# The first attention with its key and query weights multiplied on the chip, the second norm and the logits one round sooner, and more unread products between gate and experts

## The reference

```python
x = x + tanh(g_xattn[0]) * xattn0(layernorm(x), ctx)      # q = n Wq + bq, k = ctx Wk + bk, v = ctx Wv + bv
                                                          # softmax(q k^T) v, one head, width 256
x = x + tanh(g_ffn[0])   * moe(layernorm(x))              # logits of 12, the best 2; 8 experts (256 -> 512 -> 256, silu),
                                                          # 4 "zero" experts that hand the row on
x = x + tanh(g_xattn[1]) * xattn1(layernorm(x), ctx)      # 16 heads of 16, then Wo
x = x + tanh(g_ffn[1])   * fp8_linear(layernorm(x))
```

## Time and profile before

| | |
|---|---|
| three runs | 387.19, 388.37, 388.74 us |
| the profiled execution | 389.65 us |
| its span, first to last instruction | 387.8 us |
| mean granted clock of PE | 0.972 of 2.4 GHz |
| PE, DVE, ACT, POOL busy | 350.9, 266.2, 223.2, 159.3 us |

### The profile page before, as it was taken

One profiled execution on the slowest core, in us unless ns is written; L12 is line 12 of the kernel. 1 busy time (PEld: TensorE's weight loads), 2 busy tenths in 40 slices (PEclk: granted clock), 3 DMA queues, 4 the chain that ended last, 5 costly groups with the idle time before them and its releaser, 6 DMA issues.

```text
span 387.8 us, 9156 instructions
## 1 busy us (share of the span) xinstructions
PE 350.9 (90%) x2992; PEld 277.5 (72%) x2993; DVE 266.2 (69%) x678; ACT 223.2 (58%) x462; POOL 159.3 (41%) x215
## 2 busy tenths in 40 slices
PE   1989999877899999999999999889999999989874
PEld 1778787645799999999999983657666666656642
DVE  1559779893645665555544567867888998685995
ACT  2488798511444455444554442566677778737694
POOL 7397599504355555565555444321133023010000
PEclk9999999975999999999999999989999999999997
DMA  7998662301133334323232214211011000000014
GB/s 201 305 416 356 275 246 84 109 2 54 46 104 102 128 95 135 104 72 81 68 79 73 66 56 137 95 57 50 8 57 56 2 2 2 3 2 2 0 56 163
DMA packets 15387, 38.26 MB, mean 99 GB/s; under 512 B 3574, under 2 KB 4748, under 8 KB 13820
## 3 DMA queue, kind: packets, MB, share of 16 engines
q1 hardware_dynamic: 9978, 22.55, 16.6%
q0 software_dynamic: 3936, 10.45, 9.3%
q10 hardware_dynamic: 1442, 4.85, 3.2%
HBM read 24.34 MB, written 13.50 MB: 98 GB/s over the span
## 4 chain that ended last, share of the span: by engine, by line
PE 71%; DVE 10%; ACT 7%; DMA 6%; issue 3%; ACTq 1%; SPq 1%; POOL 0%; DVEq 0%
PE two L1747 14%; PE two L1760 14%; PE two L1896 5%; PE two L1926 4%; PE two L1779 4%; PE two L1961 4%; PE two L1882 4%; PE two L1862 3%; DMA x_sb<-in_x 3%; PE two L1770 2%; PE two L1953 2%; PE two L1613 1%; DMA bq_sb<-in_bq 1%; PE two L1942 1%; PE two L1630 1%
## 5 line engine op out<-in xcount | busy, mean ns | idle before, releaser
L1226 DVE SCALAR_TENSOR_TENSOR gate<-th,two 128x512 f32<-128x512 f32 x39 | 26.8, 687 | 59.6 <-ACT th L742 34.1
L742 ACT ACTIVATE th<-two 128x512 f32<-128x512 f32 x39 | 23.3, 599 | 73.0 <-PE two L1760 40.2
L549 POOL DMA_INDIRECT y_d<-y_sb,goal_i x39 | 38.5, 986 | 50.6 <-ACT y_sb L752 50.6
L543 POOL DMA_INDIRECT xg<-xn_d,slot_i x39 | 37.9, 971 | 33.5 <-DVE slot_i L1179 13.8
L1747 PE MATMUL two<-wh,gh 128*128 x156 | 44.2, 283 | 0.1
L1747 PE MATMUL two<-wh,gl 128*128 x156 | 44.0, 282 | 0.0
L1747 PE MATMUL two<-wl,gh 128*128 x156 | 43.8, 281 | 0.0
L563 POOL TENSOR_TENSOR rstd<-var,half 128x2 f32<-128x2 f32 x14 | 9.8, 701 | 76.9 <-DVE var L1293 76.9
L1326 DVE TENSOR_REDUCE nm<-two 128x8 f32<-128x960 f32 x32 | 36.1, 1152 | 5.3 <-PE two L1882 5.0
L516 POOL TENSOR_TENSOR wl<-wl,wh 128x512 fp32r<-128x512 f32 x28 | 35.3, 1278 | 8.5 <-ACT wh L671 8.5
L1760 PE MATMUL two<-wh,xh 128*128 x78 | 35.0, 449 | 1.8 <-DVE xl L1220 1.8
(11 more groups left out here) (273 smaller groups left out, 883.1 us busy)
## 6 DMA issues: line engine op xcount, KB each, us to landing
wl<-in_wmoe SPq DMA_DIRECT2D x8, 1024.0 KB, 14.4
y_d<-wh ACTq DMA_DIRECT2D x4, 1024.0 KB
yg<-y_d SPq DMA_DIRECT2D x7, 512.0 KB, 3.5
xn_d<-xq SPq DMA_DIRECT2D x8, 256.0 KB, 2.0
xz<-xn_d SPq DMA_DIRECT2D x8, 256.0 KB
out_x<-of SPq DMA_DIRECT2D x8, 256.0 KB, 2.0
x_sb<-in_x SPq DMA_DIRECT2D x1, 1024.0 KB, 11.6
x_sb<-in_x SPq DMA_DIRECT2D x1, 768.0 KB, 4.5
```

The costliest lines, as they stand in the source:

```text
L543: pool.indirect_dma_start(xg[:, n % 2, :], None, xn_d, bass.IndirectOffsetOnAxis(ap=slot_i[:, n:n + 1], axis=0)).then_inc(gathered[n % 2], 16)
L549: pool.indirect_dma_start(y_d, bass.IndirectOffsetOnAxis(ap=goal_i[:, n:n + 1], axis=0), y_sb[:, n % 2, :], None).then_inc(y_stored[n % 2] ...
L742: nc.scalar.activation(th[:], bank[2 + k][:], ACT.Tanh, scale=0.5).then_inc(th_ok, 1)
L1226: dve.scalar_tensor_tensor(gate[:, k, :], th[:], 1.0, bank[2 + k][:], ALU.add, ALU.mult).then_inc(gate_ok, 1)
```

## The change

In the first attention the key and query weights are multiplied once at the start (`fold_keys`: transpose of `wk0`, its product with `wq0` and `bq0`, and the products of the biases). `keys0` then makes the keys of all eight batches in four products of 480 columns and two of one row; DVE (`copy_kq0`) and ACT (`copy_kq1`) keep them before round 1. `keys_by_query`, `copy_kt0`, `copy_kq` and `copy_bqk` go. The loops have `B + 6` rounds (DVE's starts at -4) where they had `B + 9`; the second norm stands two or three rounds behind the attention step as before, and its logits one round nearer. The pieces of the weights are dealt out by the tables `HIGHS`, `LOWS` and `VECTOR_LOW`, and DVE takes five of the rests, not four. The transfers that clear `y_d` move from ACT's list to SP's, behind the seventh of the eight weight transfers. In routing 7 unread products come behind the last value products, one behind each of the first three groups of slot products, and 5 where 3 stood. One unread product stands in the second attention before PE waits for `oT_ok`.

```diff
-        VECTOR_LOW, VECTOR_FROM = (7, 10, 13, 16), 5
-        LOW_LATE = {B: 3, B + 1: 4, B + 2: 3, B + 3: 2, B + 4: CHUNKS}
+        HB = B // 2 * LK
+        HIGHS = 0, 2, 3, 3, 2, 2, 2, 2, 3, 3, 3, 3, 2, 2
+        LOWS = (1, 2, 2, 2, 2, 2, 2)
+        VECTOR_LOW = 2, 5, 8, 11, 13
...
                 sp.dma_start(wl[:, c].bitcast(F32), wmoe[:, c]).then_inc(chunk_in[m], 16)
+                if m == LOADS - 2:
+                    sp.wait_ge(zero_ok, 1)
+                    sp.dma_start(xn_d[0:1, :], wh[0:1, E_FFN * WE - D:].bitcast(F32)).then_inc(zeroed, 16)
+                    y_p = y_d[1:1 + 2 * TILES * P, :].rearrange("(p r) n -> p (r n)", p=P)
+                    for c in range(0, 2 * TILES * D, ZEROS):
+                        sp.dma_start(y_p[:, c:c + ZEROS], wh[:, E_FFN * WE - ZEROS:].bitcast(F32)).then_inc(zeroed, 16)
...
+            for b in range(4):
+                root0(b)
+            low_next(1)
+            root0(4)
+            root0(5)
+            for b in range(6, B):
+                low_next(2)
+                root0(b)
+            low_next(1)
+            for b in range(B):
+                if b:
+                    low_next(LOWS[b - 1])
+                root1(b)
...
-            def copy_kt0(b):
...
+            def copy_kq1():
+                act.wait_ge(fold_ok, 3)
+                for h in range(2):
+                    act.wait_ge(fold_done, 6 + h)
+                    nc.scalar.activation(keys_of_half(1, h), bank[4 + h][:, 0:HB].rearrange("p (b k) -> p b k", k=LK),
+                                         ACT.Identity, bias=kq_bias[:, 1:2]).then_inc(kq1_ok, 1)
...
-            def clear_y():
...
-            for t in range(B + 9):
-                if t == B - 1:
-                    clear_y()
...
+            for t in range(B + 6):
                 if 0 <= t - 3 < B:
...
+                    copy_probT(t - 3)
+                high_next(HIGHS[t])
+                if 0 <= t - 5 < B:
+                    norm1(t - 5)
+                if 0 <= t - 1 < B:
+                    copy_xT(t - 1)
+                if t == 1:
+                    copy_kq1()
+                if 0 <= t - 2 < B:
+                    exp0_of(t - 2)
                 if t < B:
                     norm0(t)
...
-            def copy_kq(b):
...
-            def copy_bqk(b):
...
+            def copy_fold():
+                dve.wait_ge(fold_done, 1)
+                dve.tensor_copy(wkT[:].rearrange("p c n -> p (c n)"), bank[5][:, 0:C * P]).then_inc(fold_ok, 1)
+                dve.wait_ge(fold_done, 2)
+                dve.tensor_copy(qk[:], bank[0][:, 0:D + 1]).then_inc(fold_ok, 1)
+                dve.wait_ge(fold_done, 3)
+                dve.tensor_copy(kq_bias[:, 0:C], bank[7][:, 0:C])
+                dve.tensor_copy(kq_bias[0:1, C:C + 1], bank[7][0:1, C:C + 1]).then_inc(fold_ok, 1)
+            def copy_kq0():
+                dve.wait_ge(fold_ok, 3)
+                for h in range(2):
+                    dve.wait_ge(fold_done, 4 + h)
+                    dve.tensor_scalar(keys_of_half(0, h), bank[2 + h][:, 0:HB].rearrange("p (b k) -> p b k", k=LK),
+                                      kq_bias[:, 0:1], None, ALU.add).then_inc(kq_ok, 1)
+                for h in range(2):
+                    dve.wait_ge(fold_done, 8 + h)
+                    dve.tensor_scalar(bqk[:, h * HB:(h + 1) * HB], bank[6 * h][0:1, 0:HB], kq_bias[0:1, C:C + 1], None,
+                                      ALU.add).then_inc(kq_ok, 1)
...
-            for t in range(B + 9):
...
+            for t in range(-4, B + 6):
+                if t == 0:
+                    copy_kq0()
...
+                if t == 0:
+                    stats0(4)
+                    stats0(5)
+                if 0 <= t < B:
+                    copy_v0(t)
...
+                if 0 <= t - 6 < B:
+                    logits_of(t - 6)
+                if t == B + 3:
...
+                if t == B + 4:
...
+                if 0 <= t - 4 < B:
+                    copy_xT1(t - 4)
...
+                    stats1(t - 2)
+                if 0 <= t < B:
+                    max0_of(t)
+                if 0 <= t + 4 < 4 or 6 <= t + 5 < B:
+                    stats0(t + 4 if t < 0 else t + 5)
+                if t == -4:
+                    copy_fold()
+                if 0 <= t - 1 < B:
+                    add_x1(t - 1)
+                if 0 <= t - 1 < len(VECTOR_LOW):
+                    low(VECTOR_LOW[t - 1])
...
-            def keys0(b):
...
-            def keys_by_query(b):
...
+            def fold_keys():
+                pe.wait_ge(ident_in, 16)
+                for c in range(C):
+                    ins = pe.transpose(bank[5][:, c * P:(c + 1) * P], wk0_sb[:, c * P:(c + 1) * P], ident[:])
+                ins.then_inc(fold_done, 1)
+                pe.wait_ge(wq_in, 32)
+                pe.wait_ge(fold_ok, 1)
+                for c in range(C):
+                    pe.matmul(bank[0][:, 0:D], wkT[:, c, :], wq0_sb[:, c, :], start=(c == 0), stop=(c == C - 1))
+                for c in range(C):
+                    ins = pe.matmul(bank[0][:, D:D + 1], wkT[:, c, :], bq0_sb[:, c:c + 1], start=(c == 0), stop=(c == C - 1))
+                ins.then_inc(fold_done, 1)
...
+                        pe.matmul(bank[7][:, m:m + 1], wq0_sb[:, c, m * P:(m + 1) * P], bk0_sb[:, c:c + 1], start=(c == 0),
+                                  stop=(c == C - 1))
...
+                    ins = pe.matmul(bank[7][0:1, C:C + 1], bq0_sb[:, c:c + 1], bk0_sb[:, c:c + 1], start=(c == 0),
+                                    stop=(c == C - 1))
+                ins.then_inc(fold_done, 1)
+            def keys0():
+                pe.wait_ge(fold_ok, 3)
+                for m in range(C):
+                    for h in range(2):
+                        pe.matmul(bank[2 + 2 * m + h][:, 0:HB], qk[:, m * P:(m + 1) * P], ctxT_sb[:, h * HB:(h + 1) * HB],
+                                  start=True, stop=True).then_inc(fold_done, 1)
+                pe.wait_ge(set_up, 1)
+                transpose_x0(0)
+                for h in range(2):
+                    pe.matmul(bank[6 * h][0:1, 0:HB], qk[:, D:D + 1], ctxT_sb[:, h * HB:(h + 1) * HB], start=True,
+                              stop=True).then_inc(fold_done, 1)
...
-            for t in range(B + 9):
+            fold_keys()
+            keys0()
+            for t in range(B + 6):
+                if t == B + 2:
+                    pe.wait_ge(con_in, IN_CON)
+                if 0 <= t - (B + 2) < 3:
+                    products1(t - (B + 2), t - (B + 1))
                 if 0 <= t - 5 < B:
...
+                    transpose_x1(t - 5)
+                if 0 <= t - 2 < B:
+                    transpose_prob(t - 2)
+                if 0 <= t - 1 < B:
+                    scores0(t - 1)
+                if 0 < t < B:
+                    transpose_x0(t)
+                if 0 <= t - 2 < B:
+                    attend(t - 2)
+                if t == 0:
+                    pe.wait_ge(wv_in, 32)
+                if t < B:
+                    values0(t)
+                if t == 6:
...
+                if 0 <= t - 6 < B:
+                    gate_of(t - 6)
...
             products1(8, len(P1))
+            pe.wait_ge(split_h, 1)
+            busy(bank[5], 7)
             for n in range(4):
...
+                if n < 3:
+                    busy(bank[5], 1)
             pe.wait_ge(split_d, len(VECTOR_LOW))
-            busy(bank[5], 3)
+            busy(bank[5], 5)
             pe.wait_ge(blocks_kept, 1)
             e0, e1 = experts(0), experts(1)
             busy(bank[5], 3)
             scores_by_key(B - 1, 0)
             transpose_o(B - 2, 1)
+            unread(1, D, 0)
```

More of the change, by code:

```diff
@@ L181, in build @@
         rsum = sb("rsum", [P, U], F32, att)
-        kt0 = sb("kt0", [P, 2, C, LK], F32, att)
+        wkT = sb("wkT", [P, C, P], F32, att)
+        qk = sb("qk", [P, D + 1], F32, att)
+        kq_bias = sb("kq_bias", [P, C + 1], F32, att)
         xq = sb("xq", [P, 2, U * D], F32, att)
@@ L518, in _, with low_next @@
             pieces = iter(j for j in range(CHUNKS) if j not in VECTOR_LOW)
[L520 to L537 removed]
+            def low_next(n):
+                for j in itertools.islice(pieces, n):
+                    low(j)
+            for b in range(4):
[11 more added lines that the diff above has]
+                root1(b)
+            for j in pieces:
+                low(j)
             pool.wait_ge(slots_kept, 1)
@@ L620, in _ @@
             act.wait_ge(ctx_in, IN_CTX)
-            def copy_kt0(b):
-                act.wait_ge(kt_done, b + 1)
-                wait(act, kq_done, b - 1)
-                for m in range(C):
-                    ins = nc.scalar.activation(kt0[:, b % 2, m, :], bank[5][:, m * LK:(m + 1) * LK], ACT.Identity,
-                                               bias=bk0_sb[:, m:m + 1])
-                ins.then_inc(kt_ok, 1)
+            def copy_kq1():
[4 more added lines that the diff above has]
```

(24 more changed lines are left out.)

125 lines of the change are left out of this document (13 added, 112 removed).

## The result

| kernel | median of the runs (lowest to highest), us | ratio to before, 95% interval |
|---|---|---|
| before | 386.94 (386.08 to 388.74, 6 runs) | |
| changed | 391.86 (390.89 to 394.10, 6 runs) | 1.0136 [1.0113, 1.0159] |

The changed kernel is slower by 1.4%, 4.9 us; 390.8 us was predicted, but as +2.4 on a base of 388.37. The six runs of the kernel before have their median at 386.94. The profiled execution of the changed kernel took 393.3 us with a span of 391.4, 1.4 above its median.

What follows compares the result with a forecast made beforehand. Transfers set the pace to about 21 us, then a nearly gapless PE to the last logits. A stall of +3.0 and routing's -0.6 gave +2.4 on 388.37, 390.8 us; range 382.3 to 394.0.

Steps and rivals of the forecast that it cites:

- The round: First attention: the change takes 2.01 us of PE's 5.62 us round, leaving 3.6; a full round is 4.9.
- the rival without a stall: First attention: stores pass the zeros or land by 45.6, last logits 5.1 us earlier, total 382.4; chance 0.22.
- The store behind the zeros: SP's queue: batch 0's store stands behind 4 x 1024 KB of zeros, landing at 52.2, so norm1(2) waits; chance 0.52.
- ACT stands from 45.6 to 52.2: First attention: ACT reaches norm1(2) at 45.6 and waits until batch 0's store lands at 52.2.
- +3.0 on the last logits: End of first attention: the stall moves the last logits from 74.2 to 77.2, +3.0 us.
- the late landing of `wf`: SP's queue: `wf`, last ahead of the zeros, landed at 41.4 before; 10.2 us of zeros follow, to 51.6.
- the case that the late part catches up: SP's queue: lower bound for the store's landing, 49.6; as half a stall, total say 387, chance 0.16.
- the order within the queue: SP's queue: descriptors within one ring are consumed in order, so stores stand behind all the zeros; whole forecast turns on it.
- Routing: Routing, after the last logits: denser unread products were put at -0.6 us.
- POOL's rests ... end some 5 us before the gathers; 0: Routing: POOL's 27 weight rests, 8 behind the last root, end some 5 us before the gathers and cost 0.
- The quarter of 2.4 us: Routing: full PE clock from the unread products on would save 2.4 us; a quarter was taken, -0.6.
- the bounds of -2.4 and +2.4: Routing: -2.4 us if PE runs at full speed, at most +2.4 if the seven unread products run at 1.2 GHz.

Runs made afterwards that it cites:

- e5: Changed kernel, one transfer of zeros behind each of the first four stores and POOL's last eight rests cut to 16 columns: 383.96 us, ratio 0.9907.
- e9: Changed kernel, zeros behind the first four stores, last eight POOL rests in quarters, two unread products in round 1, first POOL root sooner: 382.88 us.
- e1: Changed kernel, the four zero transfers placed one behind each of the stores of batches 0 to 3: 390.11 us, ratio 1.0092.
- e2: Changed kernel, POOL's last eight weight rests cut from 512 to 16 columns, that computation left out: 385.71 us, ratio 0.9963.
- e7q: Changed kernel, each of POOL's last eight rests done in four instructions of 128 columns, same data: 389.06 us, ratio 1.0056.
- e10: Changed kernel, POOL's root of norm1(0) put ahead of the rest that stood before it: 394.57 us, ratio 1.0180.
- e6: Changed kernel, zeros behind stores, three POOL rests before each of the last two roots, two more on DVE, four last in quarters: 391.20 us.
- e7s: The combination e6 with two unread products of 256 columns added in round 1: 390.50 us, ratio 1.0072 to the kernel before.

## Why the prediction came out right, and where it did not

- **The round.** `max` came at 23.54 (predicted 23.7), 27.59, 33.52, 38.22, 43.07: the fifth started at 43.07, and was to end at 42.6. The round of 5.93 holds the stretch at 1.2 GHz. The next has no idle time on DVE and took 4.70, where its list with a `stats0` was put at 4.9; PE's part alone took 3.64 (`v` from 29.61 to 33.25), where 3.6 was put. The one of 4.85 (4.3 by DVE's list) holds a gap of PE of 1.46 us for the first `norm1`, which had waited for POOL. Right in the main. e5 and e9 are some 4 us under the kernel before, less than the 5.9 of the rival without a stall, which had no waits of DVE in it.
- **The store behind the zeros.** The mechanism is right (e1: 2.0 us to landing once the zeros are out of the way). The term was mis-sized: "ACT stands from 45.6 to 52.2" was 47.4 to 50.0, and +3.0 on the last logits were +1.41, in which are also DVE's waits (1.2 by e2) and the clock at the start (about 1.2). I had added the zeros to the late landing of `wf` in the earlier trace rows; the store landed 0.3 from the lower bound that I gave for the case that the late part catches up (49.6). By the medians the stall is worth 1.75 us. That there would be a stall, in that place, rested on the order within the queue, and e1, e7q and e10 bear it out.
- **Routing.** Predicted -0.6, measured +3.4 on the way from the last logits to the first expert product. The step that failed is "POOL's rests ... end some 5 us before the gathers; 0". They do end early, 12 us before; but they were priced by who waits for them, and not by who works beside them. By e2 the rests cost 6.15 us of the medians, more than the whole loss of 4.9: without them the change would have gained.
- **The unread products.** The quarter of 2.4 us was a guess between the two levels of the clock. In the profiled execution they gained nothing; in six others with the same list about 0.9 us. Both lie within the bounds of -2.4 and +2.4. The seven products, which ran at 1.2 GHz, brought the first slot product 0.2 us later (0.95 behind `onerow` in place of 0.74). The medians can't tell.
- **The total.** The sign is right. That 390.8 lies so near 391.86 is luck. The forecast change was +2.4 and the measured one +4.9; the base of three runs, 388.37, was 1.4 above the median of six, which hid more than half of the miss. And inside the change two errors went against each other: a stall too large (2.6 us for 6.6; on the last logits all terms together are 1.6 off), and a loss of 2.86 on the way to `pairs` that was put at 0.

## What to carry to other kernels

Work that is moved out of the way on one engine lands beside other work: for every long chain of GpSimd instructions ask which VectorE steps now run at the same time, and look in the trace for small steps whose duration, not whose idle time, is out of line with their columns. If they can't be parted, cut the long instructions; quarters of the same data gave back 2.8 us here. A large transfer that nobody waits for is put behind the small ones in its queue, not ahead of them. And before a difference of two traces is put down to an edit, look whether a third trace that has the edit, and one that hasn't, show it too: the clock behind PE's gaps differed here between executions of nearly the same list.

## What the runs showed of the hardware

- A VectorE instruction with both operands in SBUF waits for the GpSimd instruction that is running, here a subtraction of two operands in SBUF: 48 columns took 0.21 us alone, mostly 0.95 to 1.19 beside rests of 1.25, 0.21 to 0.38 beside rests of 0.46, and the slow ones ended 0.05 to 0.07 behind the POOL instruction. Beside the same rests a reduction with one operand took 0.20 and a step with an operand in PSUM (`logit`) 0.18. A TENSOR_SCALAR with one operand (`prod`) took 0.42 beside rests and 0.20 without. The Trainium skill (SBUF — State Buffer, Who interferes with whom) states this: the two engines share a pair of ports as an exclusive lock for a whole instruction, which a VectorE step with two SBUF inputs takes. The runs agree, and e7q is the case that parts a lock from a shared rate. It holds both ways (in e6 POOL's three rests took 4.17 beside DVE's rest, in place of 3.75).
- A store of 256 KB behind zeros in the same queue took 8.6, 10.00 and 11.7 us to land in three traces, and 2.0 ahead of them (e1). The Trainium skill (DMA: Bandwidth & Descriptors, Queues, rings and completion order) says that descriptors within a ring are consumed in order, which is what the forecast took from it; e1 agrees.
- In the changed kernel the granted clock fell to 0.50 some time behind gaps of PE of 1.18 us (at the start) and 1.33 us (ahead of 51.16). It stayed at 1.00 where two unread products left 0.31 of the first (e7s, e9), but also in e7q, where the gap was 1.17. Behind a gap of 2.0 us with five unread products ahead of it, PE was at 2.4 GHz in six traces and at 1.2 GHz in the changed kernel's. The length of the gap alone doesn't decide.
